# O^T scratch in longer runs, half-tile splits off GpSimd, earlier raw weights and last store in an attention-plus-experts kernel

## The reference

```python
xn = layernorm(x)
Q, K = xn @ Wq[h] + bq[h], xn @ Wk[h] + bk[h]      # 16 heads, each Q1|Q2 and K1|K2 of 64
P = softmax(Q1 K1^T / 8) - lam * softmax(Q2 K2^T / 8)
O = P @ (xn @ Wv[h] + bv[h])
attn = 0.2 * (layernorm(concat(O) @ Wo + bo) * gamma + beta)
e = argmax(xn @ switch_w + switch_b)               # one of 8 experts for each token
ffn = max_prob * (gelu(xn @ w1[e] + b1[e]) @ w2[e] + b2[e])
out = x + attn + ffn
```

## Time and profile before

| | us |
|---|---|
| median of 3 runs | 1843.43 |
| lowest, highest | 1838.34, 1845.68 |
| profiled execution, its own time | 1841.33 |
| its span, first to last instruction | 1839.5 |
| PE busy | 1789.6 (97%) |
| DVE, ACT, POOL busy | 1538.1, 1409.6, 663.9 |
| mean DMA rate | 233 GB/s |

### The profile page before, as it was taken

The page is one execution under the profiler, slowest core; times in us unless marked ns, Lnnn a source line. Parts: engine busy times, 40 slices in busy tenths (PEclk is TensorE's granted clock), DMA queues, the critical chain, the costliest instruction groups (busy, mean ns, idle before and its releaser), DMA issues. The chain is left out here.

```text
span 1839.5 us, 32514 instructions
## 1 busy us (share of the span) xinstructions
PE 1789.6 (97%) x10474; PEld 1392.6 (76%) x10474; DVE 1538.1 (84%) x2636; ACT 1409.6 (77%) x3358; POOL 663.9 (36%) x717
## 2 busy tenths in 40 slices
PE   5999999999999999999999999999999999999997
PEld 4777777777777777777777777777677699999997
DVE  3988898899889888988898889888999866887467
ACT  4898888888888888888888888888788776676422
POOL 2444222222222222223222222222237455556554
PEclk8999999999999999999999999999999999999899
DMA  7899988888888888888888888888877586667698
GB/s 232 228 247 251 247 226 220 224 236 219 218 226 237 224 222 228 233 223 218 235 232 214 212 234 225 220 218 231 227 206 185 177 311 230 241 234 269 199 361 282
DMA packets 212915, 427.77 MB, mean 233 GB/s; under 512 B 28080, under 2 KB 107952, under 8 KB 206736
## 3 DMA queue, kind: packets, MB, share of 16 engines
q1 hardware_dynamic: 207744, 411.20, 80.1%
q0 software_dynamic: 4688, 13.51, 2.2%
q10 hardware_dynamic: 320, 1.05, 0.2%
HBM read 175.17 MB, written 49.15 MB: 122 GB/s over the span
## 5 line engine op out<-in xcount | busy, mean ns | idle before, releaser
L609 ACT ACTIVATE e<-p_score,nmax 128x512 f32<-128x512 f32 x1024 | 697.1, 688 | 134.1 <-DVE nmax L956 132.7
L475 POOL TENSOR_SCALAR e<-e,rrec,lam 128x512 f32<-128x512 f32 x512 | 394.0, 770 | 981.5 <-DVE rrec L923 981.0
L956 DVE TENSOR_REDUCE nmax<-p_score 128x2 f32<-128x1024 f32 x512 | 622.8, 1216 | 149.9 <-PE p_score L1101 145.8
L1101 PE MATMUL p_score<-ks,qs 128*128 128x512 f32 x2048 | 581.2, 406 | 13.8 <-ACT e L609 9.4
L1101 PEld LDWEIGHTS p_score<-ks,qs 128*128 128x128 f32 x2048 | 366.4, 189 | 184.6 <-issue 62.2
L1064 PE MATMUL p_proj<-xh,w 128*128 128x512 f32 x1024 | 386.2, 418 | 4.5 <-DVE xl L682 1.6
L930 DVE SCALAR_TENSOR_TENSOR pm<-e,rrec 128x512 f32<-128x512 f32 x512 | 382.8, 748 | 0.4 <-POOL e L475 0.2
L561 ACT COPY pT<-p_tr 128x512 f32<-128x512 f32 x512 | 301.7, 589 | 101.6 <-PE p_tr L1113 101.3
L1113 PE MATMUL p_tr<-consts,pm 128*128 128x128 f32 x2048 | 308.5, 273 | 1.7 <-ACT pT L561 1.6
L1113 PEld LDWEIGHTS p_tr<-consts,pm 128*128 128x128 f32 x2048 | 249.2, 140 | 80.2 <-issue 20.1
L1130 PE MATMUL p_pv<-pT,v 128*64 128x512 f32 x1024 | 247.7, 605 | 0.7 <-ACT pT L561 0.7
(11 more groups left out here) (211 smaller groups left out, 1832.9 us busy)
## 6 DMA issues: line engine op xcount, KB each, us to landing
ks<-k_parts SPq DMA_DIRECT2D x508, 256.0 KB, 4.8
qs<-q_parts SPq DMA_DIRECT2D x512, 128.0 KB, 4.3
w<-weight_parts_scratch SPq DMA_DIRECT2D x56, 1024.0 KB, 10.5
w<-in_w SPq DMA_DIRECT2D x46, 1024.0 KB, 7.1
oT_parts_scratch<-oT SPq DMA_DIRECT2D x32, 512.0 KB, 6.1
op<-oT_parts_scratch SPq DMA_DIRECT2D x32, 512.0 KB, 8.9
wv<-weight_parts_scratch SPq DMA_DIRECT2D x56, 256.0 KB, 5.5
weight_parts_scratch<-w SPq DMA_DIRECT2D x8, 1024.0 KB, 5.8
```

Source lines behind the costliest of these rows:

```text
L475: nc.gpsimd.tensor_scalar(e2, e2, rrec[:, g % 4, 1:2], lam[:, 0:1], ALU.mult, ALU.mult).then_inc(s_e2, 1)
L609: nc.scalar.activation(ex[:, g % EX, m, :], p_score[g % 2][:, m, :], ACT.Exp, bias=nmax[:, g % 2, m:m + 1], accum_out=rsum[:, g % 4, m:m + ...
L956: vec.tensor_reduce(nmax[:, g % 2, :], p_score[g % 2][:, :, :], AXX, ALU.max, negate=True).then_inc(s_max, 1)
L1101: last_op = nc.tensor.matmul(p_score[g % 2][:, m, :], qs[j][u][:, m, qt * P:(qt + 1) * P], ks[j][u][:, m, part, :], start=(part == 0), sto ...
```

## The change

The scratch for O^T gets a layout of [partition, group of 256 tokens, pair, (part,) 256 tokens], so that one group of one partition is a run of 4 KB (whole) or 8 KB (parts); the buffers in SBUF follow, `load_parts` becomes one DMA, and its stores write runs of 1 KB (whole, 2 KB before) and 2 KB (parts, as before). PE goes through the pairs of a group from the last to the first and waits for the split whole ones only midway. The bias and the store of the last tile come before `low_o(1)` and before `load_whole(2)`; `load_parts(1)` comes before `load_parts(2)`; POOL adds beta to x tiles 2 and 3 between fetches. For tiles 16 to 21 the low part of w2 is made by DVE (`w2_low`) and not by POOL, one half of the next w1's high part by ACT. `WO_FROM` is 7, and two more turns are written out. At the start, `keep_warm` issues 12 and 8 transposes whose result nobody reads; `high_v(0)` and `high_v(1)` come sooner on ACT and `high_v(2)` at step 3; SP takes half of the spread of k0; raw weights of pair 2 are loaded before the spreads of q1 and k1.

```diff
+WARM = (12, 8)
@@ SP, front stage
             spread(0, "q", 0)
+            sp.wait_ge(s_lo, 2)
+            spread_by(sp, 0, "k", 0, (1,))
+            sp.wait_ge(s_wvhi, 1)
+            load_raw_v(2)
+            load_raw(2)
             for what in "qk":
                 spread(1, what, 0)
+            sp.wait_ge(s_wvhi, 2)
+            load_raw_v(3)
             for n in range(PER_BATCH, 2 * PER_BATCH):
                 load_x(n)
-            load_raw(2)
-            for pair in (2, 3):
-                load_raw_v(pair)
@@ POOL
-                if g == 1:
+                if g == 4:
                     low_v(2)
@@ ACT
+            high_v(0)
             high_part(0, "q0")
             high_part(0, "k0")
             act.wait_ge(s_lo, 2)
-            spread_by(act, 0, "k", 0)
-            high_v(0)
+            spread_by(act, 0, "k", 0, (0,))
...
+            high_v(1)
             scale_q(1)
             high_qk(1, 0)
             high_qk(1, 1)
-            high_v(1)
...
-                if g == 0:
+                if g == 3:
                     high_v(2)
@@ PE
             pe.wait_ge(s_const, 16)
+            keep_warm(WARM[0])
             for n in range(PER_BATCH):
                 transpose_x(n)
+            keep_warm(WARM[1])
@@ stores of O^T (and the copies into oT alike)
-                    sp.dma_start(oW_d[h, :, a:b], oT_whole).then_inc(s_ost, 16)
+                    sp.dma_start(oW_d[:, a:b, h, :], oT_whole).then_inc(s_ost, 16)
-                    sp.dma_start(oP_d[h - WHOLE, :, :, a:b], oT[:, :, :].bitcast(F32)).then_inc(s_ost, 16)
+                    sp.dma_start(oP_d[:, a:b, h - WHOLE, :, :], oT[:, :, :, :].bitcast(F32)).then_inc(s_ost, 16)
@@ experts
-        WO_FROM = 9
+        WO_FROM = 7
-        LOOP_END = PAIR_TILES // 2 - 4
+        LOOP_END = PAIR_TILES // 2 - 5
@@ POOL
-                if n == 0:
+                if n == 0 or PAIR_TILES <= n < FFN_TILES - 1:
                     continue
@@ ACT, in tile n (16 to 21), group 2
+                    if g == X_AT + 1 and t.half_follows():
+                        act.wait_ge(s_w1[1 - j], 16 * (t.half_next + 1))
+                        act.wait_ge(s_h, HG * n)
+                        nc.scalar.copy(w1p[1 - j][:, 0, 1, :], w1[1 - j][:, 1, :]).then_inc(s_w1hi_act, 1)
@@ DVE, before the four groups of tile n
+                early = t.half_follows()
+                if early:
+                    w1_high(n + 1, 1 - j, t.half_next, 0, False)
+                if t.exact and t.fs_before == 1 and t.fs == 1:
+                    w2_low(n - 1)
@@ SP, output
-                for c in range(2):
-                    sp.dma_start(op[n % OPS][:, c, WHOLE:PAIRS, :].bitcast(F32), oP_v[:, c, :, n * G:(n + 1) * G]
-                                 ).then_inc(s_op[n % OPS], 16)
+                sp.dma_start(op[n % OPS][:, WHOLE:PAIRS, :, :].bitcast(F32), oP_d[:, n, :, :, :]
+                             ).then_inc(s_op[n % OPS], 16)
...
+            load_parts(1)
             load_parts(2)
-            load_parts(1)
+            store(FFN_TILES - 1, 0, 1)
             load_whole(2)
-            store(FFN_TILES - 1, 0, 1)
@@ DVE, output
-            for n in range(OPS):
+            low_o(0)
+            add_b2(FFN_TILES - 1, 0, LOOPED // 2, False, 1)
+            for n in range(1, OPS):
                 low_o(n)
-            add_b2(FFN_TILES - 1, 0, LOOPED // 2, False, 1)
@@ PE, output
-                pe.wait_ge(s_op[c], 32 * (n // OPS + 1))
-                pe.wait_ge(s_olo, n + 1)
...
-                    for k in range(PAIRS):
+                    for k in range(PAIRS - 1, -1, -1):
+                        if s == 0 and k == PAIRS - 1:
+                            pe.wait_ge(s_op[c], 16 * (n // OPS + 1))
+                        if s == 0 and k == WHOLE - 1:
+                            pe.wait_ge(s_olo, n + 1)
@@ scratches
-    oW_d = nc.dram_tensor("oT_whole_scratch", [WHOLE, P, T], F32).ap()
-    oP_d = nc.dram_tensor("oT_parts_scratch", [PAIRS - WHOLE, P, 2, T], F32).ap()
+    oW_d = nc.dram_tensor("oT_whole_scratch", [P, GROUPS, WHOLE, GROUP], F32).ap()
+    oP_d = nc.dram_tensor("oT_parts_scratch", [P, GROUPS, PAIRS - WHOLE, 2, GROUP], F32).ap()
```

More of the change, by code:

```diff
@@ L294, in front_stage, with spread_by @@
         HALF = KT * 2 * P
-        def spread_by(queue, u, what, pair):
+        def spread_by(queue, u, what, pair, maps=range(2)):
             j = pair % 2
             src = parts[what][u]
-            for m in range(2):
+            for m in maps:
                 a = src[m * D:(m + 1) * D]
@@ L1028, in group_pair, with keep_warm @@
                 return PAIRS * (n // PER_BATCH - 1) + X_PAIRS[n % PER_BATCH]
+            def keep_warm(count):
+                for _ in range(count):
+                    nc.tensor.transpose(p_tr[:, 0, :], ident, ident)
             def ranks():
@@ L1323, in ffn_and_output_stage, with w2_low_done @@
         LOOPED = FFN_TILES - 1
-        LOOP_END = PAIR_TILES // 2 - 4
+        LOOP_END = PAIR_TILES // 2 - 5
         assert LOOPED % 2 == 0 and PAIR_TILES % 2 == 0
+        def w2_low_done(engine, n):
+            if isinstance(n, int) and n >= PAIR_TILES:
+                engine.wait_ge(s_w2lo_half, n - PAIR_TILES + 1)
+            else:
+                engine.wait_ge(s_w2lo, n + 1)
         def op_free(engine, n):
@@ L1358, in x_in_middle, with half_follows @@
                 return self.exact and self.has(1) and (self.n == 0 or self.fs_next == 1)
+            def half_follows(self):
+                return self.exact and self.fs == 1 and self.has(1)
             def second(self):
@@ L1407, in body @@
                     sp.wait_ge(ahead.s_last_lo, 1)
-                    sp.dma_start(oP_d[PAIRS - 1 - WHOLE, :, :, T - S:T], ahead.oT[:, :, :].bitcast(F32)).then_inc(s_oT, 16)
+                    sp.dma_start(oP_d[:, GROUPS - PER_BATCH:GROUPS, PAIRS - 1 - WHOLE, :, :],
+                                 ahead.oT[:, :, :, :].bitcast(F32)).then_inc(s_oT, 16)
                     first_of_output()
@@ L1519, in _ @@
             pool.wait_ge(s_w2lo_dve, 1)
-            for n in range(R):
-                add_beta(n)
+            add_beta(0)
+            add_beta(1)
             pool.wait_ge(s_st[0], 16 * (LOOPED // 2 + 1))
@@ L1525, in _ @@
                 fetch(n)
+                if n in (1, 2):
+                    add_beta(n + 1)
                 if n >= R:
@@ L1566, in body @@
                     act.wait_ge(s_oT, 16 * (B * PAIRS - 1))
-                    nc.scalar.copy(ahead.oT[:, 0, :], ahead.p_last[:, :]).then_inc(ahead.s_last_hi, 1)
+                    nc.scalar.copy(ahead.oT[:, :, 0, :], ahead.p_last[:, :].rearrange("p (g s) -> p g s", s=G)
+                                   ).then_inc(ahead.s_last_hi, 1)
             def output_weights(n):
@@ L1582, in high_o @@
                 op_free(act, n)
-                nc.scalar.copy(op[n % OPS][:, 0, 0:WHOLE, :], of[n % 2][:, :, :]).then_inc(s_ohi, 1)
+                nc.scalar.copy(op[n % OPS][:, 0:WHOLE, 0, :], of[n % 2][:, :, :]).then_inc(s_ohi, 1)
             turns(body, after=output_weights)(act)
@@ L1627, in w1_low, with w2_low @@
             def w1_low(n, j, k):
-                dve.wait_ge(s_w1hi, KT * n + k + 1)
+                halves = max(n - PAIR_TILES, 0) if isinstance(n, int) else 0
+                if halves and k == 1:
+                    dve.wait_ge(s_w1hi_act, halves)
+                else:
+                    dve.wait_ge(s_w1hi, KT * n + k + 1 - max(halves - 1, 0))
                 v.tensor_tensor(w1p[j][:, 1, k, :], w1[j][:, k, :], w1p[j][:, 0, k, :].bitcast(F32),
                                 ALU.subtract).then_inc(s_w1lo, 1)
+            def w2_low(n):
+                dve.wait_ge(s_w2hi, n + 1)
+                v.tensor_tensor(w2p[n % 2][:, 1, :, :], w2[n % 2][:, :, :], w2p[n % 2][:, 0, :, :].bitcast(F32),
+                                ALU.subtract).then_inc(s_w2lo_half, 1)
             def add_b2(n, j, half, fresh, fs):
@@ L1662, in body @@
                     if t.has(1) and not t.first() and not t.second():
-                        if g < KT:
+                        if g < KT and not early:
                             w1_high(n + 1, 1 - j, t.half_next, g, not t.after(1))
-                        else:
+                        if g >= KT:
                             w1_low(n + 1, 1 - j, g - KT)
@@ L1818, in outputs @@
             def outputs(n, j, fresh, fs, last=False):
-                pe.wait_ge(s_w2lo, n + 1)
+                if last:
+                    pe.wait_ge(s_w2lo, PAIR_TILES + 1)
+                else:
+                    w2_low_done(pe, n)
                 pe.wait_ge(s_hlo, HG * (n + 1))
@@ L1851, in _ @@
                     nc.tensor.matmul(p_o[r][:, s, :], ones_r[:, :], bop[:, :], start=True, stop=False)
-                    for k in range(PAIRS):
+                    for k in range(PAIRS - 1, -1, -1):
[3 more added lines that the diff above has]
+                            pe.wait_ge(s_olo, n + 1)
```

(4 more changed lines are left out.)

35 lines of the change are left out of this document (17 added, 18 removed).

## The result

| | before | after |
|---|---|---|
| median of the runs | 1842.76 us (4 runs, 1838.34 to 1845.68) | 1819.45 us (4 runs, 1818.67 to 1821.61) |
| ratio, 95% interval | | 0.9877 (0.9855 to 0.99) |
| profiled execution, its span | 1841.33, 1839.5 us | 1818.79, 1817.0 us |
| DMA packets, of them under 2 KB | 212915, 107952 | 196277, 91312 |

The account below looks back on a forecast made before the run. PE, busy 97% of the span, was held up at the start, the end of the experts and the DMA-bound output; -10.5 - 1.5 - 2.3 - 9.5 = -23.8 us from 1841.33 gives 1817.5, forecast 1818, range 1808 to 1831.

Parts of the forecast that it names:

- Start: First 60 us: earlier loads, split spread of k0 and warm clock save 10.5 us, bounds 7 and 14.
- (a): Start: high_v(2) at step 3 and its load sooner remove ACT's wait, exponential of step 1 at 31.8 us, 7.6 us gained.
- (b): Start: the spread of k0 issued by two queues gains 1.5 us, between 0 and 2.5.
- (c): Start: 12 and 8 extra transposes in idle PE time raise the clock for q0 and k0, 1.3 us, at most 2.4.
- (e): Start: DMA work squeezed into about 49 us takes time back, set against the end of PE's cold stretch; no separate size.
- start rival: Packed loads land late and PE waits at steps 8 to 16; start gains only 5.5 us, total 1823; chance 0.15.
- Half tiles: End of experts: w2's low part moved off POOL shortens the period from 9.52 to 9.2 us, -1.5 us over five tiles.
- Clock: Last expert tile: half of a 4.6 us loss at low clock is saved, -2.3 us, between 0 and -4.6.
- Output: Output stage: longer runs and earlier loads bring groups from 6.39 to 5.8 us, -9.5 us, bounds -5 and -12.2.
- rate rival: Output stage: long runs don't raise the DMA rate, HBM sets it; groups stay at 6.4 us, about 1825; chance 0.15.
- share under 0.97: Output stage: sign of a right forecast, DMA share below 0.97 at a higher rate per share.
- pitch rival: Output stage: reads at a pitch of 128 KB slow the O^T loads, 1899 us at half the rate; chance 0.03.

Follow-up runs that it names:

- u_start: Changed kernel with its whole start part undone (no warm transposes, old orders, high_v(2) at step 0); median 1823.54 us.
- n_warm: Changed kernel without its 20 warming transposes at the start; median 1820.5 us.
- s_mid: Changed kernel with the store of pair 0's weight parts issued right behind the spreads of q1 and k1, ahead of raw V weights 3 and x loads; median 1818.71 us.
- s_qk4: Changed kernel with ACT's high_qk(2, 0) moved from step 2 to step 4, order of DMAs unchanged; median 1818.15 us.
- u_half: Changed kernel with the low part of w2 in half tiles on POOL again and both halves of the next w1's high part on DVE; median 1824.51 us.
- u_layout: Changed kernel with the old layout of the O^T scratch and buffers and two DMAs for the parts; median 1824.27 us.
- u_store: Changed kernel with the old order on SP, POOL and DVE where the output begins, PE keeping its new order of pairs; median 1823.96 us.
- o_layout: Kernel before with only the new layout of the O^T scratch and buffers and one DMA for the parts; median 1833.49 us.
- s_mid_again: The same kernel as s_mid, timed again with more rounds; median 1817.44 us.

## Why the prediction was right, and where it was not

**Start, -10.5 forecast, -5.6 found, below the lower bound of 7.** (u_start puts it at 4 to 5.) Part (a) did what it said: the wait for raw V weights went. But (a), (b) and (c) together were to bring the exponential of step 1 to "near 29", 10.4 us sooner, and it came at 31.28, 8.1 us sooner. Parts (b), 1.5, and (c), 1.3, gave 0.9 in arrival (almost none of it without (c): n_warm has 25.42) and nothing in the first exponential, since the four score matmuls took 2.07 us at half clock; "first scores near 23" was wrong. In all, (c) is 1.0 to 1.2 in n_warm, little more than the scatter.

The step that failed is (e), "I set these two against each other". The bill that DMA sends was seen and no row was sought for it. Between steps 2 and 3 the gain falls from 7.9 to 3.9 us. Two items are measured: `high_qk(2, 0)` behind the store of pair 0's weight parts, 4.10 us, of which s_mid and s_qk4 keep 0.7 to 1.7 at step 511 when it is moved; and the waits for `ks` that appear when it is gone. Before, ACT was late by 9 us itself, so the store had long landed (issued at 34.23, and `high_qk(2, 0)` at 42.85 waited for nothing). The question what is late next when a stall goes was answered with spreads and raw weights and not with ACT's own next wait. The start rival (-5.5, chance 0.15) is right in size and not in mechanism: it had PE waiting at steps 8 to 16, and no such wait stands in the changed kernel's trace.

**Half tiles, -1.5: right, in size and cause.** The 1.81 us operations are gone up to the last tile. The sum took 9.52 to 9.2 for five tiles; measured are 9.39 to 9.09 on average, nearly the same distance. By the Trainium skill, "SBUF — State Buffer", section "SBUF: two separate sides", the two engines share a port pair as an exclusive lock. The 1.81 and 0.41 us of the earlier trace rows agree, and so does u_half: its three long operations end 0.3 us behind the end of POOL's pass, and the two periods without one are 8.6 us.

**Clock, -2.3 forecast, -4.7 found.** I took half of a fall because its place seemed to be chance. In the profiled executions gaps of 0.45 us bring none in ten kernels, and the three kernels with the old split have one fall each, at different tiles. Not each longer gap brings one: the 1.16 us at 1681.82 in the kernel before did not. And 4.7 us is the figure of one execution. The kernel before has a mean granted clock of 0.988 to 0.995 over its 38 executions in the experiments' rounds, its four fastest at 0.994 and its seven slowest at 0.988 to 0.990, so some lose more than others. u_start, which has its start and the new half tiles, has 0.994 to 0.996.

**Output, -9.5 forecast, -8.9 found.** The mechanism held: 371 GB/s for each full share over the stage, from a forecast of 2.36 MB in 6.5 to 6.1 us, or 363 to 387, and 390 in its steady part; pace 5.89 (forecast 5.8); no wait for `op`; y stored at 1715.37, 0.9 us after group 0's start where it was 11.9, the 11 us of the forecast. The mis-sized term is PE's floor, 5.68 from one pair of halves 2.84 us apart; other pairs are 2.94 to 3.00, and 16 groups take 94.3 us. The share of the orders was too small as well: the rate rival left 2.5 us for them, and u_layout wins 5.2 us of the stage by them alone. Its gain is a head start, which the old rate has used up after nine groups. The sign "share under 0.97" failed by little, 0.98: DMA and PE are nearly even. The rate rival falls: windows between 1760 and 1800 us give 380 to 391 GB/s for each full share in the changed kernel, u_store and o_layout, and 334 or 335 in the two kernels with the old layout. By the Trainium skill, "DMA: Bandwidth & Descriptors", section "Where 436 GB/s comes from", the HBM side binds at about 358 GB/s in transfers between HBM and SBUF. The 402 GB/s over 20 us are above that, but a ninth of a group's bytes are a store; by an estimate from that the loads alone are some 357, so this stage neither breaks that figure nor shows it. The 426 GB/s of the earlier trace rows, in a window of 1 us that loads expert weights, are above it. The pitch rival falls with the higher rate: it was reached with parts at a pitch of 128 KB (the whole ones are at 64).

**Tail, 0 forecast, -1.8 found.** PE's end to the kernel's end was 10.0 and is 8.2. DVE's last half comes 2.0 us after PE's end, and 3.8 before:

```profile
1810.76 0.16 DVE L1815 TENSOR_SCALAR omom<-omom 128x2 f32<-128x2 f32 x1
```

```profile
1833.30 0.16 DVE L1771 TENSOR_SCALAR omom<-omom 128x2 f32<-128x2 f32 x1
```

It is 9.1 to 10.0 in u_layout, u_store and o_layout, which speaks for the load of DMA, but 9.7 in u_half, and 8.4 and 9.1 in s_mid and s_mid_again, which are one kernel; its cause stays open.

The total was right to 1.5 us because 4.9 us too much in the start and 0.6 in the output stood against 2.4 and 1.8 us too little in clock and tail. The sum of errors is no merit of the steps.

## What to carry to other kernels

When a stall of an engine goes, list that engine's next waits in program order and ask of each whether its transfer lands before the new time; the stalled time had been hiding them. Where the DMA engines were full, each reorder of issues tried here traded one wait for another, and none won more than some 2 us. Read a stall's cost tile by tile and not from an average: the tiles that escape it show what it costs. Look at two parts of one stage both alone and together: here the layout alone won 4.3 us of the stage, the orders alone 5.2, both 8.9, and only both brought the stage to PE's bound.

## What the runs showed of the hardware

Longer runs raised the DMA rate for each full share from 334 to 390 GB/s, with two thirds of the bytes in runs of 4 and 8 KB instead of 1; o_layout, which changes nothing else but the number of DMAs for the parts, has 384 in the same window. PE fell to half clock for some 10.2 us, each time 2.4 to 2.7 us after the end of a gap of 0.87 (before, o_layout) or 1.16 us (u_half) between half tiles, though not behind every such gap, and not once in the profiled executions where the gaps were 0.45. A DVE operation with both operands in SBUF took 0.41 us alone, and 1.8 to 2.1 where it started during POOL's pass over w2, ending 0.3 us behind it. A clock raised by 20 extra transposes was lost again in one wait of 4.80 us: the projections ended 1.4 us sooner (19.74 and 21.16), the first exponential came 0.5 sooner (27.91 and 28.39). In the full queue SP's four DMAs of one spread took 2.4 us to issue at one time and 5.53 at another:

```profile
22.79 2.41 SPq L305 DMA_DIRECT2D qs<-q_parts  x4
34.76 5.53 SPq L305 DMA_DIRECT2D qs<-q_parts  x4
```
